# Adding four product banks into two by an accumulating DMA, and moving one bank of layer 3 from VectorE to ScalarE, in a compressed interaction network

## What is computed

```
out[n, o, e] = relu(sum over i, j of  xi[n, i, e] * x0[n, j, e] * W[i, j, o]  + b[o])
z = sum over e of concat(x0, out1, out2, out3)
y = relu(relu(concat(z, ctx) @ W_top1 + b1) @ W_top2 + b2) @ W_top3
```

## Time and profile before

| | |
|---|---|
| median of 3 runs | 2486.8 us (2486.18 to 2488.17) |
| profiled execution, its own time | 2486.23 us |
| its span, first to last instruction | 2484.4 us |
| mean granted clock of PE | 0.983 of full |
| busy: PE, DVE, ACT, POOL | 2388.0, 2208.1, 1976.3, 2018.3 us |

### The profile page before, as it was taken

How to read it: one execution, slowest core, us unless ns; L and a number is a source line. 1 busy time by engine, 2 the same in 40 slices (tenths; PEclk the granted TensorE clock), 3 DMA queues, 4 the chain that set the end, 5 groups by cost and what they waited for, 6 DMA issues and landing times.

```text
span 2484.4 us, 66691 instructions
## 1 busy us (share of the span) xinstructions
PE 2388.0 (96%) x13149; PEld 1326.8 (53%) x13149; DVE 2208.1 (89%) x9242; ACT 1976.3 (80%) x7182; POOL 2018.3 (81%) x2009
## 2 busy tenths in 40 slices
PE   1599999999999999999999999999999999999998
PEld 0355555555555555555555555555555555555553
DVE  4399999999999999999999999999999999999995
ACT  1388888888888888888888888888888888888874
POOL 7488888888878888888778888888877777777773
PEclk6799999999999999999999999999999999999999
DMA  4000000000000000000000000000000000000000
GB/s 165 9 12 12 11 10 11 11 11 9 9 10 11 11 11 11 12 11 10 9 9 11 11 10 11 11 11 11 9 10 9 9 8 9 10 9 9 9 10 3
DMA packets 113450, 34.35 MB, mean 14 GB/s; under 512 B 107860, under 2 KB 111575, under 8 KB 113400
## 3 DMA queue, kind: packets, MB, share of 16 engines
q1 hardware_dynamic: 107256, 30.73, 5.3%
q0 software_dynamic: 6144, 3.16, 0.8%
HBM read 12.82 MB, written 0.00 MB: 5 GB/s over the span
## 4 chain that ended last, share of the span: by engine, by line
PE 94%; DVE 1%; issue 0%; DMA 0%; ACT 0%; SPq 0%; DVEq 0%
PE y L411 79%; PE m L401 11%; PE m L392 3%; DVE acc L672 1%; PE m L466 0%; PE y L473 0%; PE y L466 0%; DMA xT<-lo 0%; DVE ends L672 0%; PE y L479 0%; DVE msum L681 0%; DVE ends L686 0%; DVE pooled L725 0%; SPq L249 0%; DVE acc L668 0%
## 5 line engine op out<-in xcount | busy, mean ns | idle before, releaser
L411 PE MATMUL y<-whi,xT 128*128 128x512 f16 x6144 | 1990.7, 379 | 11.2 <-DMA xT<-lo 8.1
L503 ACT ACTIVATE work<-y,xc 128x128 f32<-128x128 f32 x5632 | 1611.3, 372 | 394.5 <-PE y L411 367.0
L672 DVE SCALAR_TENSOR_TENSOR acc<-y,xc,acc 128x128 f32<-128x128 f32 x5632 | 1669.4, 342 | 83.4 <-PE y L411 78.4
L311 POOL TENSOR_TENSOR part<-part,work 128x512 f32<-128x512 f32 x896 | 1137.5, 1270 | 214.9 <-ACT work L503 132.8
L411 PE MATMUL y<-wlo,xT 128*128 128x512 f16 x3072 | 1165.3, 379 | 0.0
L411 PEld LDWEIGHTS y<-whi,xT 128*128 128x128 f16 x6144 | 601.3, 98 | 623.8 <-issue 10.2
L401 PEld LDWEIGHTS m<-wsq,work 128*128 128x128 f32 x2560 | 388.6, 193 | 93.9 <-ACT work L523 1.9
L411 PEld LDWEIGHTS y<-wlo,xT 128*128 128x128 f16 x3072 | 300.9, 98 | 249.9 <-issue 0.8
L401 PE MATMUL m<-wsq,work 128*128 128x128 f32 x2560 | 391.2, 276 | 1.1 <-ACT work L523 1.1
L307 POOL TENSOR_TENSOR part<-work 128x512 f32<-128x512 f32 x256 | 326.6, 1276 | 62.2 <-ACT work L503 57.7
L272 POOL DMA_INDIRECT emb<-tbl,ids_sb x192 | 196.8, 1025 | 44.3 <-issue 26.6
(11 more groups left out here) (81 smaller groups left out, 958.1 us busy)
## 6 DMA issues: line engine op xcount, KB each, us to landing
xT<-hi SPq DMA_TRANSPOSE x256, 2.2
xT<-lo SPq DMA_TRANSPOSE x256, 2.4
emb<-tbl,ids_sb POOLq DMA_INDIRECT x192, 2.4
xx<-w SPq DMA_DIRECT2D x4, 768.0 KB, 8.9
work<-w SPq DMA_DIRECT2D x4, 768.0 KB, 15.0
x0T<-x0hl SPq DMA_TRANSPOSE x128
wt_sb<-W_top SPq DMA_DIRECT2D x1, 768.0 KB
w1s<-w_pair SPq DMA_DIRECT2D x1, 640.0 KB
```

The lines of the kernel that those rows point to most:

```text
L311: pool.tensor_tensor(a[:], a[:], p[:, m, :], ALU.add).then_inc(s, 1)
L411: ins = nc.tensor.matmul(dst[:], xT[layer][:, parity, a, :], w[layer][:, cols], start=i == 0, stop=i == 2)
L503: nc.scalar.activation(prods[layer][:, a, k * P:(k + 1) * P], bank[:, k * P:(k + 1) * P], ACT.Copy, scale=xc[layer][:, parity, j:j + 1]).t ...
L672: ins = nc.vector.scalar_tensor_tensor(dst, y, col, mine, ALU.mult, ALU.add)
```

## The change

1. Banks. `TAKES` goes from ADADADADADAD and DADADADADADD to AADADADADADD and DADADADADADA. In layer 2 ACT has banks 0, 1, 3, 5, 7, 9 in place of 0, 2, 4, 6, 8, 10. In layer 3 ACT has banks 1, 3, 5, 7, 9, 11 (places 13, 15, ..., 23), six in place of five, and DVE six in place of seven.
2. Sums. For each tile and layer POOL issues one DMA, when four A banks are there, that adds products 2 and 3 to products 0 and 1 in SBUF (128 partitions x 1024 float32). POOL adds products 4 and 5 into `part`, waits for the DMA, and then adds products 0 and 1. `SUMS` goes from n + 1 to n - 1 steps.
3. ACT's wait before it overwrites products is for the whole last sum, in every bank.
4. On DVE the merge of layer 3 goes from place 5 to place 10, and the pieces of layer 1 (`pre1`, `scale`, `lo_part` with `over_e`) and `x0_scale` one place later, since D banks there have other numbers. On ACT `relu(0)` goes from place 4 to 5, `hi_part` and `columns` of layer 1 from 8 to 9.
5. POOL's loop over pairs of steps is written out.

```diff
-TAKES = ("ADADADADADAD", "DADADADADADD")
+TAKES = ("AADADADADADD", "DADADADADADA")
...
-SUMS = [n + 1 for n in NA]
+SUMS = [n - 1 for n in NA]
...
+                written(3)
+                pool.dma_start(p[:, 0:2, :], p[:, 2:4, :], accum_op=ALU.add).then_inc(s_dma[layer], 16)
                 wait(pool, s, done)
-                written(1)
-                pool.tensor_tensor(a[:], p[:, 0, :], p[:, 1, :], ALU.add).then_inc(s, 1)
-                for m in range(2, NA[layer]):
-                    written(m)
-                    wait(pool, s, done + m - 1)
+                written(5)
+                pool.tensor_tensor(a[:], p[:, 4, :], p[:, 5, :], ALU.add).then_inc(s, 1)
+                wait(pool, s_dma[layer], (tile + 1) * 16)
+                for m in range(2):
+                    wait(pool, s, done + m + 1)
                     pool.tensor_tensor(a[:], a[:], p[:, m, :], ALU.add).then_inc(s, 1)
-                n = NA[layer] - 1
+                n = NA[layer] - 3
...
-                    end = (b + 1) * E
-                else:
-                    end = TILES - 6
-                with pool.Fori(0, (end + 1 - v) // 2) as pair:
-                    step(pair * 2 + v, 1)
-                    step(pair * 2 + v + 1, 0)
-            for v in range(TILES - 5, TILES):
-                step(v, v % 2)
+                while v < min((b + 1) * E + 1, TILES):
+                    step(v, v % 2)
+                    v += 1
...
-                wait(act, s_sum[layer], (t - 1) * SUMS[layer] + max(a, 1))
+                wait(act, s_sum[layer], t * SUMS[layer])
...
-                    if n == 4 and active(t1):
+                    if n == 5 and active(t1):
                         relu(0, t1)
...
-                    if n == 8 and active(t1):
+                    if n == 9 and active(t1):
                         hi_part(0, t1)
                         columns(0, t1, parity)
...
-                        if n == 1 and parity == 0 and active(v + 4):
+                        if n == 2 and parity == 0 and active(v + 4):
                             x0_scale(v + 4, k)
-                        if n == 5 and active(t3 - 1):
+                        if n == 4 and k == 3 and active(t1):
+                            pre1(t1, parity)
+                        if n == 8 and active(t1):
+                            scale(0, t1, k)
+                        if n == 10 and active(t1):
+                            if k == 1:
+                                lo_part(0, t1)
+                            if k == 3:
+                                over_e(0, t1)
+                        if n == 10 and active(t3 - 1):
                             if k == 0:
                                 merge(1, t3 - 1, 0)
                             if k == 2:
                                 merge(1, t3 - 1, 1)
-                        if n == 3 and k == 3 and active(t1):
-                            pre1(t1, parity)
-                        if n == 7 and active(t1):
-                            scale(0, t1, k)
-                        if n == 9 and active(t1):
-                            if k == 1:
-                                lo_part(0, t1)
-                            if k == 3:
-                                over_e(0, t1)
```

More of the change, by code:

```diff
@@ L181, in build @@
         s_fma = [sem(f"fmas{l}") for l in (2, 3)]
+        s_dma = [sem(f"products{l}_added") for l in (2, 3)]
         s_sum = [sem(f"sums{l}") for l in (2, 3)]
```

## The result

The changed kernel takes 2958.3 us (2955.4 to 2959.4), 1.189 times the time before (95% interval 1.188 to 1.191): 471 us slower. The prediction was 2770 us, slower; its range ended at 3000.

The account below looks back on a forecast made before the run. PE bounds the kernel at 18.33 us per step; the DMA's loop would make it 19.97, or 21.02 with gathers. 72 x 2.69 + 55 x 1.64 = 284 us on 2486 gives 2770 us, range 2510 to 3000.

Parts of the forecast that it names:

- a loop over POOL, DMA and merge: Each POOL sum waits for its DMA, then merge and relu follow; binds for L over 3.0 us, 2.0 with gathers.
- The loop's legs: Times from one relu(1) to the next through ACT, POOL, DMA and merge: 15.3 + L us, 16.35 + L with gathers.
- L: Landing time of the accumulating DMA: taken as 4.35 us, between bounds of 3.7 and 5.0.
- the excess over 4.03 us once more: Layer 3's DMA has 4.03 us of cover; what L has above that is added to the loop again, 0.32 us.
- DVE freer: DVE, 1 us freer in each step, matters only at the end of the kernel.
- The forecast's own range: Times for L of 3.6 to 5.1 us: 2635 to 2960 us, chance 0.53.
- DVE's run over banks 8 to 12: Bank 12's products come 0.45 us late for PE's bank 17; alone a step of 18.8 us, +57 us, but absorbed.
- PE would wait at bank 21: PE's bank 21 wants bank 16's buffer, whose last two products stand behind merge(0) on DVE.
- The signs: Profile after: PE about 690 records with gathers, 720 without; DVE's longest wait msum for psum, POOL's the add after the DMA.
- Costs of nothing: Taken as 0: ACT's wait for the whole last sum, POOL's loop written out, layer 1's later transposes, the kernel's end.
- the copy's rival: The accumulating DMA goes at a copy's rate or better, L 2.4 to 3.6 us: 2545 to 2635 us, chance 0.22.
- The rival on the other side, not slower: L under 2.0 and bank 12 done 0.45 us sooner, PE stays the bound: 2480 to 2487 us, chance 0.14.

Follow-up runs that it names:

- e1: The changed kernel with DVE's loop over pairs of steps written out, nothing else changed: 2891.0 us, ratio 1.162.
- e5: The changed kernel without the accumulating DMA, POOL adding all six products, and DVE's loop written out: 2571.4 us, ratio 1.034.
- e7: e1 with layer 2's merge moved from place 16 to 20 and all that follows from it moved later: 2712.4 us, ratio 1.090.
- e10: e1 with the first gather of a step issued behind layer 2's accumulating DMA: 2800.4 us, ratio 1.125.
- e3: The changed kernel with a plain copy of the same size in place of the accumulating DMA: 2660.3 us, ratio 1.070.
- e8: e5 with layer 3's merge moved from place 10 to 14 and over_e(2) from 11 to 16: 2581.2 us, ratio 1.038.
- e9: e5 with layer 3's merge and over_e(2) both moved to place 6: 2565.4 us, ratio 1.031.
- e11: e1 with the accumulating DMA in layer 2 alone, POOL adding layer 3's six products: 2715.1 us, ratio 1.091.
- e2: The changed kernel without the accumulating DMA, POOL adding all six products, DVE's loop kept: 2612.3 us, ratio 1.050.
- e4: e2 plus accumulating DMAs of the same size and number into an otherwise unused buffer: 2774.9 us, ratio 1.116.

## Why the prediction was right, and where it was short

- **PE stops being the bound, and the step becomes a loop over POOL, DMA and merge.** Right. The chain, the waits and e1, e5, e7 and e10 bear it out. e1 is 404 us over the kernel before; of these the DMA is worth 320, since without it the banks and the order would cost 84. Two DMAs stand in nearly every turn.
- **The loop's legs, 15.3 + L and 16.35 + L in gather steps, and the excess over 4.03 us once more.** Right to some tenths. With the measured L of 4.8 it is 20.9 and 21.9; e1 shows 20.5 to 20.9 in plain steps (704, 703 and 688 records from 2200 to 2800 us, granted clock 0.99 to 1.00) and 21.6 to 22.0 with gathers (666 and 655, clock 0.97). The wait for layer 3's DMA behind POOL's first add is there, 0.87 us where 4.8 - 4.03 gives 0.77.
- **L was the term that was mis-sized:** 4.35 taken, 4.8 measured, inside its bounds of 3.7 to 5.0. Put into the sum: 72 x (21.9 - 18.33) + 55 x (20.9 - 18.33) = 257 + 141 = 398 us in place of 284, so 2884, where e1 measured 2891. That an add lands later than a copy was reasoned rightly: e3's copy lands after 2.9. The 1.9 us between them are more than the 1.3 at which a second stream was reckoned, and that they are the second read is not shown. The Trainium skill (DMA: Bandwidth & Descriptors, Anatomy of one DMA) gives 3.2 us for that copy and the trace agrees within 0.3; the estimate with a second read from the Trainium skill (Collectives: The Full Stack, Why ReduceScatter is half of AllGather), 4.4 us, is 0.4 under what the adding DMA took.
- **A term was missing: the pass of DVE's loop,** 67 us between e1 and the change, the clock behind it included (granted 0.97 in plain steps, 0.99 to 1.00 in e1). The prediction costed "DVE freer" at nothing and looked at POOL's loop alone. 398 + 67 = 465 of the 471. That the pass costs this is shown by e1. Why it costs nothing before is not: in the trace before, the records of one pass and of the next follow each other without a wait, and DVE's first product waited 8.8 us in all. One reading is that DVE, which now has its first bank at number 2 and is 1 us freer in each step, has lost the queued work that hid the pass. But the instruction queue moved only 43 packets before and 343 now, so there may have been nothing to hide. No run tells these apart.
- **The forecast's own range, 2635 to 2960, holds 2958 by luck in part.** It was left wide for an L of up to 5.1; with L at 4.8 the sum gives 2884, and the rest of the way is the missing term.
- **DVE's run over banks 8 to 12 makes a step of 18.8.** Right in size, 18.75 in e5, and absorbed in the change. What is left of it in the change is a stop of 0.19 us at place 17. But it isn't a matter of bank 12 alone (e8, e9).
- **PE would wait at bank 21.** Right, but the prediction took it for the only place and didn't follow the ring over the end of a step: place 0 takes place 20's buffer, four places back and not five. The second loop that e11 shows runs through it. By e11's legs it would turn in 20.0 us with L of 4.8; in e1, where relu(0) stands in ACT's leg too, it took 20.7 and was on the chain in two of 25 turns. So it is close under the first, and in e11, with the first shortened, it sets the step.
- **The signs.** In e1 they are as written: DVE's longest wait is msum for psum (308.6 us, 2.4 each), POOL's is the add behind the DMA (383.8). In the change both stand second, behind DVE's first product and POOL's first add, and the records, 631 to 668 with gathers and about 669 without, are under the 690 and 720 that were given.
- **Costs of nothing.** ACT's wait for the whole last sum, the transposes and the end: no wait of that kind shows in the steps; PE's waits for the transposes of x are 8.9 us in all, 8.1 before, though one of the two now lands after 3.2 us. That POOL's loop written out costs nothing was not tested.
- **The rivals.** L of 2.9 (e3) was the copy's rival as a mechanism, 2660.3. Its legs give 19.25 us with gathers and 18.8 without, 2486 + 72 x 0.92 + 55 x 0.47 = 2578, and DVE's loop pass of 41 to 67 us makes it 2619 to 2645, 15 us or more short. The rival on the other side, not slower, would have needed an L under 2.0; no run came near it. No kernel tried is faster than the kernel before.

## What to carry to other kernels

A transfer that takes over an engine's work also puts its latency between that engine's queue and the next step; count the turn of that loop (from a merge to the same merge a step later, over each queue and the ring of buffers, past the end of the step too) before counting the work saved. On a core bound by PE, 247 us less of POOL's busy time was worth nothing and 9.3 us of waiting in each turn of 20 cost 320. Look also at the idle time before the first instructions of each pass of an engine's loop, and at the packets of the instruction queue: here a change that only moved work within VectorE's loop made its passes cost 67 us.

## What the runs showed of the hardware that was not expected

- 512 KB within SBUF landed after 4.8 us with an add and after 2.9 us as a copy, issued by GpSimd, whose issue takes 0.87 to 0.93 us.
- At a pass of VectorE's loop two idle stretches of 2.3 and 1.9 us stood in e2, and of 4.1 and 2.0 us in e4, beside 60 GB/s of accumulating DMAs; some 1.1 us of the first is the wait of a step that starts no pass. The instruction queue moved 342 to 352 packets in the four kernels after the change with that loop and 128 to 138 in the nine without, but only 43 before the change. The Trainium skill (Runtime: NRT & Kernel Launch, Instruction fetch mechanics) says that a taken branch out of the two pages held makes the engine wait for a fetch; the packets of the kernels after the change, the length under traffic and e1 agree with that. The loop before the change, with 43 packets and no wait, doesn't show it, and why it fetched so much less, no run tells.
- Beside those DMAs the first transpose landed after 3.2 us, where it was 2.2.
- TensorE ran at its lower level for about 3 us, its matmuls 0.43 us apart in place of 0.22, behind 11 of the 16 stops of 2.1 to 2.5 us that it made in the change from 2100 to 2860 us, and behind none of its stops of 1.0 to 1.2 us there. The windows show a granted clock of 0.97, where it was 1.00 before; what that is worth in time was not separated.
